# Second attention: grouped row maxima on VectorE, later transposes of them, PSUM split into four banks for maxima and two for scores

## The reference, cut to what matters

```python
q = (rms_norm(x, g) @ w_q).reshape(b, n, 16, 8)        # 16 heads of 8
k, v = ...                                             # 4 key and value heads
q, k = q * rf, k * rf                                  # a rotary factor by position
qkt = einsum('bhqd,bhkd->bhqk', q, k) / sqrt(128)
s = softmax(qkt, axis=-1) @ v                          # the row maximum is taken off first
return s + s @ w_o
# beside it: expert = argmax(xn @ router.T); each row later goes through its expert's FFN
```

## Time and profile before

| | us |
|---|---|
| median of 3 runs | 1653.48 |
| lowest and highest | 1649.02, 1654.18 |
| span of the profiled execution | 1651.9 |

### The profile page before, as it was taken

The page is one execution under the profiler, slowest core; times in us unless marked ns, Lnnn a source line. Parts: engine busy times, 40 slices in busy tenths (PEclk is TensorE's granted clock), DMA queues, the critical chain, the costliest instruction groups (busy, mean ns, idle before and its releaser), DMA issues. The chain is left out here.

```text
span 1651.9 us, 30013 instructions
## 1 busy us (share of the span) xinstructions
PE 1455.9 (88%) x9488; PEld 716.9 (43%) x9488; DVE 1180.7 (71%) x3123; ACT 946.4 (57%) x1805; POOL 833.9 (50%) x941
## 2 busy tenths in 40 slices
PE   3999999969993279999999999999999999849996
PEld 1444444469993123333333333333333332239996
DVE  3688777833334568899889998899989998514443
ACT  2565556524441147777777778777777777612221
POOL 4688888743003463556555655556565620114443
PEclk9999999979997569999999999999999999969998
DMA  1111211289995111122112221122212210347771
GB/s 38 46 56 54 64 56 49 80 242 298 304 296 145 57 56 46 56 77 73 55 55 65 78 61 54 57 75 73 59 55 62 70 51 13 108 155 239 236 241 58
DMA packets 144965, 165.76 MB, mean 100 GB/s; under 512 B 29073, under 2 KB 115217, under 8 KB 142649
## 3 DMA queue, kind: packets, MB, share of 16 engines
q1 hardware_dynamic: 92377, 74.76, 15.2%
q10 hardware_dynamic: 38608, 58.62, 11.6%
q0 software_dynamic: 13824, 30.47, 6.0%
HBM read 111.93 MB, written 51.30 MB: 99 GB/s over the span
## 5 line engine op out<-in xcount | busy, mean ns | idle before, releaser
L1592 DVE TENSOR_REDUCE c_mx<-c_ps_mx 128x1 f32<-128x512 f32 x1024 | 649.8, 683 | 89.6 <-PE c_ps_mx L1828 82.1
L1496 ACT ACTIVATE c_pt<-c_ps_e 128x512 f32<-128x512 f32 x1024 | 567.1, 601 | 189.9 <-PE c_ps_e L1798 176.3
L1798 PE MATMUL c_ps_e<-c_qst,c_kex 74*128 74x512 bf16 (+1 forms) x1024 | 347.7, 388 | 3.5 <-ACT c_pt L1496 1.9
L1811 PE MATMUL c_ps_v<-c_pt,c_vp 128*32 128x512 f32 x2048 | 274.5, 608 | 1.1 <-ACT c_pt L1496 0.7
L1333 POOL DMA_INDIRECT c_gy<-ys,mt x128 | 124.2, 970 | 276.5 <-PE c_ps_v L1811 129.9
L1828 PE MATMUL c_ps_mx<-c_kex,c_qst 64*128 64x512 bf16 x1024 | 204.6, 396 | 57.9 <-DVE c_mx L1592 40.9
L1828 PEld LDWEIGHTS c_ps_mx<-c_kex,c_qst 64*128 64x128 bf16 x1024 | 49.3, 93 | 367.8 <-DVE c_mx L1592 345.3
L998 PE MATMUL f_ps_h<-f_xT,f_w 128*128 128x256 f32 x800 | 197.0, 386 | 0.2 <-DVE f_xT L1064 0.2
L558 ACT ACTIVATE a_pt<-a_ps_s,temp 128x1024 f32<-128x1024 f32 (+3 forms) x128 | 113.1, 884 | 91.3 <-PE a_ps_s L652 86.3
L499 POOL DMA_INDIRECT xs<-a_xn,a_meta x128 | 135.6, 1059 | 38.1 <-issue 35.3
L998 PEld LDWEIGHTS f_ps_h<-f_xT,f_w 128*128 128x128 f32 x800 | 145.4, 194 | 15.9 <-issue 0.6
(11 more groups left out here) (225 smaller groups left out, 1895.0 us busy)
## 6 DMA issues: line engine op xcount, KB each, us to landing
f_w<-in_we ACTq DMA_DIRECT2D x80, 321.0 KB, 4.4
f_w<-in_we ACTq DMA_DIRECT2D x37, 576.0 KB, 4.5
c_qst<-qparts SPq DMA_DIRECT2D x75, 192.0 KB
f_x<-rows SPq DMA_DIRECT2D x40, 257.0 KB, 3.9
f_x<-xs SPq DMA_DIRECT2D x80, 128.0 KB, 4.4
ys<-f_y ACTq DMA_DIRECT2D x80, 128.0 KB, 4.3
qparts<-c_qp SPq DMA_DIRECT2D x16, 384.0 KB, 2.5
x<-in_x SPq DMA_DIRECT2D x16, 256.0 KB, 3.0
```

What stands on the lines that cost most here:

```text
L1496: nc.scalar.activation(pt[:, s % 4, hl, :], ps_e[:, e_bank(64 * b + n)], ACT.Exp, scale=QSCALE).then_inc(exp_done, 1)
L1592: nc.vector.tensor_reduce(mx[:, g % 2, col:col + 1], ps_mx[:, m_bank(64 * b + 2 * m + par)], AX, ALU.max).then_inc(mx_done, 1)
L1798: nc.tensor.matmul(ps_e[:, e_bank(64 * b + n)], kex[rows, p, k_head(hl), kt * P:(kt + 1) * P], qst[rows, p, q_head(g, hl), :], start=True, ...
L1811: last = nc.tensor.matmul(ps_v[32 * hl:32 * (hl + 1), :], vp[:, p, kt, hl, :], pt[:, s % 4, hl, :], start=kt == 0, stop=kt == NT - 1)
```

## The change

PSUM is dealt out anew: four banks for maxima, two for scores. The two reductions of a pair become one, over two banks. The `shifts` leave DVE: POOL splits a group's maxima into two bf16 terms (`split`), PE brings both over in one bf16 matmul, ACT writes them negated. `normalise` leaves DVE too: ACT copies each group's heads out of `ps_j` (`token_copy`), DVE takes all reciprocals of a batch at once (`inverses`), POOL multiplies (`normalise`). `x1` and `xn` are written straight into four row buffers, so that `keep_x1`, `keep_xn` and two small copies go, and the token number comes from an `iota` on POOL. On PE, V moves ahead of S2, and several of the tasks through `ps_j` change their step.

```diff
-RING = 3
+RING = 2
+ROWS = 4
-def m_bank(n):
-    return n % RING
+def m_banks(n):
+    return slice(n % 2 * 2, n % 2 * 2 + 2)
-        ps_mx = ps("c_ps_mx", [P, RING, L])
+        ps_mx = ps("c_ps_mx", [P, 4, L])
 POOL
+                def normalise(i, o):
+                    pool.wait_ge(rcp_ready, b + 1)
+                    pool.wait_ge(sT_ps, b)
+                    nc.gpsimd.tensor_tensor(sall[:]..., raw[:]...[:, :, 0:DH1], rcp[:]..., ALU.mult).then_inc(all_ready, 1)
+                def split(i, o, g):
+                    pool.wait_ge(mx_done, 8 * (4 * b + g + 1) + 2)
+                    nc.gpsimd.tensor_copy(mxp[:, g % 2, 0], mx[:, g % 2]).then_inc(split_steps, 1)
+                    nc.gpsimd.tensor_tensor(mxp[:, g % 2, 1], mx[:, g % 2], mxp[:, g % 2, 0], ALU.subtract).then_inc(split_ready, 1)
                 def body(i, o):
+                    if not prev or not nxt2:
+                        split(i, o, 1)
                     combine(ln, i, o + 2); v_rows(i, o + 1)
-                    keep_xn(i, o)
+                    normalise(i, o - 1)
                     norms(ln, i, o + 2)
+                    split(i, o, 2)
                     normal_rows(i, o + 2)
+                    tokens(i, o + 2)
...
+                    split(i, o, 3)
...
 ACT
+                def token_copy(i, o, g):
+                    act.wait_ge(ot_ps, 4 * b + g + 1)
+                    nc.scalar.activation(raw[:, :, g], ps_j[:]...[:, :, :, 0:DH1 + 1], ACT.Copy).then_inc(ot_sb, 1)
+                def shifts(i, o, g):
+                    act.wait_ge(mt_ps, 4 * b + g + 1)
+                    nc.scalar.activation(shb[:, g % 2, :], ps_j[0:2 * NT * HL, 0:P], ACT.Copy, scale=-1.0).then_inc(sh_ready, 1)
                     for s in range(16):
                         exps(i, o, s, 0)
-                        if s == 7 and nxt2:
+                        if s == 2 and prev:
+                            token_copy(i, o - 1, 3)
+                        if s in (7, 11, 15):
+                            token_copy(i, o, s // 4 - 1)
+                        if s in (6, 10):
+                            shifts(i, o, s // 4 + 1)
+                        if s == 14 and nxt:
+                            shifts(i, o + 1, 0)
+                        if s == 8 and nxt2:
                             xT_copy(i, o + 2)
                         for hl in range(1, HL):
                             exps(i, o, s, hl)
+                            if s == 1 and hl == 1:
+                                shifts(i, o, 1)
+                            if s == 9 and hl == 1 and nxt2:
+                                prj_copy(i, o + 2, 1)
                         if s > 0 and s % 4 == 0:
                             ov_copy(i, o, s // 4 - 1)
-                        if s == 7 and nxt2:
+                        if s == 8 and nxt2:
                             prj_copy(i, o + 2, 0)
-                        if s == 9 and nxt2:
-                            prj_copy(i, o + 2, 1)
-                        if s == 13 and nxt2:
+                        if s == 12 and nxt2:
                             qT_copy(i, o + 2)
 DVE
-                    for par in range(2):
-                        nc.vector.tensor_reduce(mx[:, g % 2, col:col + 1], ps_mx[:, m_bank(64 * b + 2 * m + par)], AX,
-                                                ALU.max).then_inc(mx_done, 1)
+                    nc.vector.tensor_reduce(mx[:, g % 2]...[:, :, m % 8], ps_mx[:, m_banks(32 * b + m)], AX, ALU.max).then_inc(mx_done, 1)
 PE
-                    pe.wait_ge(exp_done, 64 * b + n if b or n else 1)
+                    pe.wait_ge(exp_done, 64 * b + n + 1)
-                    pe.wait_ge(mx_done, 64 * b + 2 * m + 1)
+                    pe.wait_ge(mx_done, 32 * b + m + 1)
-                    nc.tensor.transpose(ps_j[:, 0:P], mx[:, g % 2, :], k.ident[:]).then_inc(mt_ps, 1)
+                    pe.wait_ge(split_ready, 4 * b + g + 1)
+                    nc.tensor.matmul(ps_j[0:2 * NT * HL, 0:P], mxp[:, g % 2]..., k.ident_b[:], ...).then_inc(mt_ps, 1)
                     for s in range(16):
                         scores(i, o, s, 0)
                         maximum(i, o, s, 0)
-                        if s == 7 and nxt2:
-                            free = x_rows(free, i, o + 2)
+                        if s == 1:
+                            free = max_columns(free, i, o, 1)
+                        if s in (8, 9) and nxt2:
+                            free = project(free, i, o + 2, s - 8)
                         scores(i, o, s, 1)
-                        scores(i, o, s, 2)
                         values(i, o, s - 1)
+                        scores(i, o, s, 2)
                         maximum(i, o, s, 1)
                         scores(i, o, s, 3)
-                        if s in (0, 4, 8):
+                        if s in (5, 9):
                             free = max_columns(free, i, o, s // 4 + 1)
...
-                        if s in (5, 10, 14):
-                            free = token_rows(free, i, o, s // 5 - 1 if s < 14 else 2)
+                        if s in (6, 10, 14):
+                            free = token_rows(free, i, o, s // 4 - 1)
                         if s == 7 and nxt2:
-                            free = project(free, i, o + 2, 0)
-                        if s == 9 and nxt2:
-                            free = project(free, i, o + 2, 1)
+                            free = x_rows(free, i, o + 2)
...
-                        if s == 13 and nxt2:
-                            free = q_columns(free, i, o + 2)
```

192 lines of the change are left out of this document (93 added, 99 removed).

## The result

| | before | after |
|---|---|---|
| median of the runs, us | 1653.83 | 1699.16 |
| lowest and highest | 1649.02, 1654.84 | 1698.31, 1700.41 |
| ratio, 95% interval | | 1.0275 [1.0254, 1.0295] |
| span of the profiled execution | 1651.9 | 1697.5 |

A forecast was written before the change was run, and what follows sets the result against it. PE and DVE were taken as both nearly full, PE rarely held up by DVE. 30.4 (batches 1 to 13) + 4 + 4 + 1.3 = 39.7 us made the span 1691.6, the median 1693; 8-in-10 range 1657 to 1714.

The forecast's parts named there:

- The ring of two score banks: In each step S0 waits for an exponential on ACT: at least 3.04 us a step, though PE needs 2.82.
- Step 15: Last step of a steady batch, without transposes by fours or a projection behind S3: 3.04 us.
- The late steps of the last batch: Batch 15's eight steps without maxima: 2.89 us each instead of 2.40, together +4 us.
- The projections: In steps 8 and 9 PE stalls ahead of both projection halves, about 0.9 and 1.1 us, until ACT copies end.
- Steps 8 and 9: The two steps with half a projection each: 9.50 us together, where the work without waits is 7.46.
- (c): POOL late for `s_rows` or `split`, so PE waits in step 3 or 5: about 1708 us; chance 0.11.
- (d): Gaps in steps 8 and 9 let the granted clock fall: 2.5 us more a batch, 1730 us; chance 0.05.
- The ends: First and last batches: +4 in batch 0, +4 in batch 15's late steps, +1.3 after the last exponential.
- Batch 0: PE stands still some 5 us for group 1's `split` on POOL: +4 us, between -2 and +9.
- quicker maxima: Faster maxima ahead of batch 0's wait for `split`, counted only as that batch's lower bound, -2 us.
- (a): DVE was the limit and the score ring does not bite: batch 51.5 us, time 1635; chance 0.14.
- (b): Ring holds but projections do not stall, as ACT runs earlier: batch 52.7 us, time about 1660; chance 0.08.

The follow-up runs named there:

- Experiment 1: Two runs of the changed kernel with ACT's copies ahead of the projections moved earlier, first one copy, then both: 1679.23 and 1668.47 us.
- b2: Kernel before with four banks for maxima and two for scores, the grouped reduction, and V moved ahead of S2: 1665.28 us.
- f1: Changed kernel with three and three banks, single reductions, V behind S2 and both copies ahead of the projections moved earlier: 1669.59 us.
- h1: f1 with M0 behind S1, the first projection at the end of step 8 and its copy directly behind that step's exponentials: 1658.42 us.
- g4: Kernel before with a single edit on PE, M0 behind S1 instead of between S0 and S1: 1645.12 us.
- e2: e1 with `xT_copy` also moved on ACT ahead of the first exponential of step 8: 1668.47 us.
- e1: Changed kernel with the first `prj_copy` moved on ACT from the end of step 8 to behind that step's second exponential: 1679.23 us.
- g7: b2 with both maxima pairs moved behind S3 on PE: 1771.67 us.
- e3: Changed kernel with three banks each for scores and maxima and single reductions again, all else kept: 1723.54 us.
- e4: Changed kernel with PE's order in a step made S0, S1, V, S2, S3, M0, M1: 1713.85 us.
- b1: Kernel before with only the four and two banks and the grouped reduction: 1741.33 us.
- g5: e4 with both copies ahead of the projections moved earlier and `inverses` on DVE ahead of the reductions of step 2: 1660.01 us.

## Why the prediction was right, point by point

**The ring of two score banks: right in mechanism and size.** Forecast 3.04 bare, 3.26 with transposes, 3.72 with the output projection; from V to V the trace has 3.04, 3.26 and 3.72. Step 15 was 0.08 longer than forecast, steps 5 and 13 0.04, step 1 0.03. ACT has taken DVE's place in the view of waits, as forecast. The rule of the Trainium skill named in the prediction ("Perfetto Trace Analysis", Optimization Strategy) agrees with these traces: with two banks the repeated wait for a bank appears, 246 times in nearly eight batches or 17.6 us a batch, where the batch of the earlier trace rows has 4.1 in 18 waits. One sign did not come out: DVE was to have idle time ahead of nearly every reduction, and had it ahead of 100 of 248. The late steps of the last batch, forecast 2.89, in the changed kernel's timeline:

```profile
1464.83 1.06 PE L1832 MATMUL c_ps_v<-c_pt,c_vp 128*32 128x512 f32 x8
...
1467.71 1.07 PE L1832 MATMUL c_ps_v<-c_pt,c_vp 128*32 128x512 f32 x8
```

**The projections: right, a little small.** Forecast gaps of 0.93 and 1.13, measured 0.94 and 1.05, ended by the copies named. Steps 8 and 9 took 9.77 from S0 to S0, not 9.50: half a projection behind a stall cost 0.76 instead of 0.68, and ACT came 0.1 us later than summed. This, with steps 1, 5, 13 and 15, is the 0.5 us by which a steady batch (55.6) misses 55.1, or 6 us in all. Experiment 1 shows that the stalls are real, and that they were the largest term: 31 us with all that went with them, 25 by themselves.

**POOL and the clock: rivals (c) and (d), both priced at nothing in the sum, and both came in a few batches.** In one of the three slow batches (from 983.6) PE waited 1.28 us for POOL's product ahead of the transposes, after POOL had waited 3.48 for its gather. That is the event of rival (c). The other two are the event of rival (d), the granted clock at 0.50 behind the waits of step 9. The prediction priced it at 2.5 us in every batch; it cost 1.6 in two of thirteen. Together such batches cost 4.6 us over thirteen of 55.6; before had 1.2 of its own, none of it with a lower clock.

**The ends.** Batch 0 was forecast at +4. From the first pair of maxima to the first `ranks` it came at +0.5 (87.8 us against 87.2), though its gap was larger than forecast (row of the changed kernel, then the stretches around it):

```profile
597.55 0.26 PE L1914 MATMUL c_ps_j<-ident_b,c_mxp 128*32 128x128 bf16 x1 [6.97 <-POOL c_mxp L1446]
```
```profile
590.00:602.00 12.00, 5.03 (x18) 0.90 (x17) 2.29 (x3) 2.20 (x6) 11.46 (x13) 0.50 0.26 75
602.00:612.00 10.00, 9.46 (x51) 2.40 (x51) 9.57 (x26) 7.65 (x14) 1.88 (x6) 0.99 0.31 96
```

The mis-sized term is the pairs ahead of the first batch, which the forecast knew only as a bound ("quicker maxima", -2). PE has nothing but maxima to do there and DVE sets the pace: they followed each other by 1.40 us before and by 1.13 after (PE's timelines, before and then after):

```profile
566.84 0.61 PE L1828 MATMUL c_ps_mx<-c_kex,c_qst 64*128 64x512 bf16 x2 [0.79 <-DVE c_mx L1592]
568.24 0.61 PE L1828 MATMUL c_ps_mx<-c_kex,c_qst 64*128 64x512 bf16 x2 [0.79 <-DVE c_mx L1592]
```
```profile
565.44 0.61 PE L1849 MATMUL c_ps_mx<-c_kex,c_qst 64*128 64x512 bf16 x2 [0.53 <-DVE c_mx L1654]
566.57 0.61 PE L1849 MATMUL c_ps_mx<-c_kex,c_qst 64*128 64x512 bf16 x2 [0.52 <-DVE c_mx L1654]
```

From the first of these sixteen pairs to the last it is 18.9 us instead of 23.8, so 4.9 less, a little more than the forecast missed. b2, which has only the banks and the grouping, takes 18.7, and f1, with the relief but three banks, 24.2: it is the banks and the grouping, not the relief. The last batch itself was 6.2 longer, of which 3.9 are its eight late steps (forecast 4) and 1.9 the drain, from the last V to the output projection (6.59 against 4.67; forecast +1.3). The last 2.2 us lie behind it, in and around the second expert FFN, which takes 184.5 to 187.5 us in the fourteen traces.

**Luck in the number.** The forecast of the span, 1691.6, is 5.9 us under 1697.5, but the parts miss by more and partly cancel. The fourteen distances of `ranks` gave 39.8 us and not 30.4, so 9.4 too little was forecast: about 5 by the size of a steady batch, 3.4 by the slow batches just named, 0.7 by batch 14, which was put at nothing. The last batch gave 6.2 and not 5.3, and 2.2 came behind it. Against that, batch 0 took 3.5 less than forecast, and the first pair of maxima started 3.1 us earlier, ahead of anything that the forecast was about. The steady mechanism was right, with 2.3 us a batch forecast and 2.8 measured. That the total came within 6 us owes something to luck.

**The rivals.** (a) DVE was the limit and the ring does not bite: refuted by the batches of 55.6 us and by ACT ahead of the scores. Nor does relief gain with three banks: the first part is 24.21 in f1 against 24.30 before, and 24.00 in both h1 and g4. (b) no stalls: refuted by the rows; a kernel made so, e2, ran 1668 where 1660 was forecast for it. (c) and (d) came as told above, one batch and two.

The forecast wrote +2.3 a batch for stalls and ring together. The runs split the +2.8 into 2.7 for the place of the projections (V7 to V10, 13.03 against b2's 10.30), 0.6 for banks and V (b2 against before), 0.2 in the third part, and a gain of 0.8 in the first that relief and later tasks bring with four banks (22.88 against 23.67) and not with three. Of the 2.7, e1 and e2 show 1.8 as stalls behind two copies; that the other 1.0 is the place of the projections too was not tested with two score banks.

## What to carry to other kernels

When PSUM banks move from one ring to another, work out for both rings the loop that closes them: hand-off, the consumer's queue ahead of it, hand-off back, and what the producer does in between. Put the consumer's other work, its copies, into the loop as well. A ring of two was cheap when the producer's longest other work lay where the consumer was busy, and cost 76 us more when it did not, because then the consumer's copies lengthened the loop. Relief of an engine pays only in the steps in which someone waits for it: compare the steps one by one, not the busy shares. And a small copy that frees a shared bank belongs on an engine whose queue at that point has nothing long ahead of it; three of the largest losses here (the projections, the transposes of the normalised sums, the shifts in g7) came from a small copy or product in the wrong place of an engine that had time enough. Before a loss is explained by waits alone, look at the granted clock batch by batch: over 800 us its mean read 1.00 in the changed kernel, and two falls of 1.6 us each were in it.

## What the runs showed of the hardware

- A grouped reduction of 128 x 1024 out of two PSUM banks takes 1222 ns, two in a row 2.36 us, so 1.13 each; two single ones of 512 start 0.60 apart. Back to back, grouping saves about 0.07 us a pair. Where each pair waits for its matmuls, grouping and the fourth bank together saved 0.27, and no run here has one without the other. The Trainium skill ("Perfetto Trace Analysis", Optimizing Scalar/DVE Operations) gives about 125 ns for each DVE operation on PSUM; the 0.07 measured here, one start saved, is about half of that.
- In batch 0 of the changed kernel the granted clock was 0.50 (the 1.2 GHz level) ahead of the gap of 6.97 us, through it and up to 602 us, and 0.99 from there. At the lower level a score matmul took 0.61 us instead of 0.39 and V 1.9 instead of 1.07.
- In steady batches the clock fell too: in 2 of 13 behind waits of 0.94 and 1.05 us (in the changed kernel, and in e3), in 9 of 13 behind waits like that of 1.31 (e4), in none of 13 in before, b1, b2, e1, e2, f1, g4, g5 and h1. A fall cost 1.5 to 1.6 us in the changed kernel and e4.
